# One unread product of the identity ahead of the waits of every piece in a kernel's first edge loop on TensorE

## What is computed

```python
agg = jax.ops.segment_sum(x[src], dst, num_segments=N)
deg = jax.ops.segment_sum(jnp.ones_like(src, dtype=x.dtype), dst, num_segments=N)
mean = agg / jnp.maximum(deg, 1.0)[:, None]
out = mean @ W_l.T + b_l + x @ W_r.T
...
out = jax.nn.relu(out)
```

## Time and profile before

| | |
|---|---|
| time of 3 runs, median (lowest to highest) | 8019.0 us (8017.02 to 8020.97) |
| the profiled execution's own time | 7943.43 us |
| its span | 7941.6 us |
| mean granted TensorE clock over the span | 0.796 |

### The profile page before, as it was taken

One profiled execution on the slowest core, in us unless ns is written; L12 is line 12 of the kernel. 1 busy time (PEld: TensorE's weight loads), 2 busy tenths in 40 slices (PEclk: granted clock), 3 DMA queues, 4 the chain that ended last, 5 costly groups with the idle time before them and its releaser, 6 DMA issues.

```text
span 7941.6 us, 116432 instructions
## 1 busy us (share of the span) xinstructions
PE 5394.5 (68%) x23625; PEld 3970.9 (50%) x23625; DVE 5453.7 (69%) x13210; ACT 2600.2 (33%) x9112; POOL 3724.1 (47%) x3988
## 2 busy tenths in 40 slices
PE   6265666625777776946655555899577777777798
PEld 4143333323444443425555555787455555555687
DVE  8776667776666765546666666764688778778666
ACT  1022222212332231314444444211445554555211
POOL 0266666626666663645555555000444444444211
PEclk8566666766877877967777877999788888888899
DMA  3132333223333432443333333354455555555311
GB/s 109 51 89 82 91 88 89 82 82 109 107 108 112 117 110 83 137 124 111 110 111 107 109 109 110 124 163 132 120 139 140 138 139 138 140 141 139 88 43 38
DMA packets 448815, 865.10 MB, mean 109 GB/s; under 512 B 78232, under 2 KB 284168, under 8 KB 447626
## 3 DMA queue, kind: packets, MB, share of 16 engines
q0 software_dynamic: 194048, 574.45, 26.3%
q1 hardware_dynamic: 237674, 251.25, 10.2%
q10 hardware_dynamic: 16416, 31.99, 1.2%
HBM read 718.55 MB, written 298.46 MB: 128 GB/s over the span
## 4 chain that ended last, share of the span: by engine, by line
PE 30%; DVE 22%; issue 14%; another core or an unknown queue 6%; POOL 3%; SPq 3%; DMA 2%; DVEq 2%; ACT 2%; ACTq 1%; POOLq 0%
PE ps L839 6%; PE ps L1553 4%; PE ps L1818 3%; DVE big L1488 3%; PE ps L1781 3%; SPq L1411 2%; PE ps L2007 2%; PE ps L2024 2%; PE ps L1503 2%; DVE big L1911 2%; DVE big L1927 2%; DVE big L1936 1%; DVE big L786 1%; PE ps L1201 1%
## 5 line engine op out<-in xcount | busy, mean ns | idle before, releaser
L839 PE MATMUL ps<-ring 128*128 x3528 | 1479.7, 545 | 962.0 <-DVE ohb L776 410.9
L839 PEld LDWEIGHTS ps<-ring 128*128 128x128 f32 x3528 | 724.6, 251 | 1457.0 <-issue 1419.8
L1503 PE MATMUL ps<-big,ring 128*128 128x128 f32 x4928 | 875.6, 346 | 599.5 <-DVE big L1478 405.8
L746 POOL DMA_INDIRECT ring<-xl_d,idx x832 | 847.6, 1019 | 715.4 <-DVEq L641 316.0
L813 ACT CAST ring<-ohb 128x128 f32<-128x128 bf16 x1764 | 524.3, 298 | 2003.3 <-DVE ohb L776 1192.7
L1439 POOL DMA_INDIRECT big<-x_d,idx x832 | 793.9, 954 | 747.9 <-ACT ring L1464 506.4
L1503 PEld LDWEIGHTS ps<-big,ring 128*128 128x128 f32 x4928 | 802.5, 250 | 672.5 <-DVE big L1478 455.7
L1689 POOL DMA_INDIRECT ring<-kv_d,gidx x754 | 712.8, 945 | 814.0 <-issue 746.9
L746 POOL DMA_INDIRECT ring<-x_d,idx x832 | 827.7, 995 | 438.2 <-issue 232.7
L776 DVE TENSOR_SCALAR ohb<-iotab,keyf,nbase 128x128 bf16<-128x128 bf16 x1764 | 571.0, 324 | 462.6 <-remote 161.4
L786 DVE TENSOR_TENSOR big<-big,ps 128x257 f32 (+1 forms) x1764 | 754.1, 428 | 170.1 <-issue 108.1
(11 more groups left out here) (413 smaller groups left out, 9283.0 us busy)
## 6 DMA issues: line engine op xcount, KB each, us to landing
bas_d<-big SPq DMA_DIRECT2D x1232, 128.0 KB
att_d<-wreg SPq DMA_DIRECT2D x464, 132.0 KB
big<-bas_d SPq DMA_DIRECT2D x49, 1024.0 KB, 5.6
x_d<-ring SPq DMA_DIRECT2D x147, 128.0 KB, 1.7
gh_d<-aside ACTq DMA_DIRECT2D x49, 384.0 KB
ring<-xl_d,idx POOLq DMA_INDIRECT x832
ring<-x_d,idx POOLq DMA_INDIRECT x832
big<-x_d,idx POOLq DMA_INDIRECT x832
```

The lines of the kernel that those rows point to most:

```text
L746: nc.gpsimd.indirect_dma_start(out=rows[:, j, :], out_offset=None, in_=table, in_offset=bass.IndirectOffsetOnAxis(ap=idx_of(c), axis=0)).t ...
L839: T.matmul(ps[k][:, 0:D], ohf[:, k, :], rows[:, slot, :].rearrange("p a d -> p (a d)"), start=True, stop=True)
L1503: last = nc.tensor.matmul(ps[j % 8][:, 0:FW].rearrange("p (n h b) -> p n h b", n=NB, h=H)[:, :, h, :], xs[:, j, h * P:(h + 1) * P], wts[:, ...
```

## The change

In the first edge loop (`layer` is 0) TensorE makes one product of the identity with itself, 128 x 128 in f32, into bank `ps[7]`, ahead of the waits of each piece. Nothing reads it, and it increments no semaphore. The second edge loop keeps `gates_pe` in that place.

```diff
@@ -830,6 +830,8 @@
                     of[:min(GRP, NQ - q)] = load_group(mybir.EngineType.PE, chunk_i, q, min(GRP, NQ - q), NCK - 1)
                 if layer:
                     gates_pe(pe, q)
+                else:
+                    T.matmul(ps[7][:, 0:P], ident[:, :], ident[:, :], start=True, stop=True)
                 pe.wait_ge(e["oh"], layer * NQ + q + 1)
                 pe.wait_ge(e["arrived"], of[a] + layer * NCK + 1)
                 if past(q, G1):
```

## The result

| | before | after |
|---|---|---|
| median of 8 runs (lowest to highest) | 8023.41 us (8017.02 to 8027.39) | 8043.49 us (8036.59 to 8049.11) |
| the profiled execution's own time | 7943.43 us | 8043.77 us |
| its span | 7941.6 us | 8041.9 us |
| its mean granted clock | 0.796 | 0.810 |

The ratio of the medians is 1.0025, with a 95% interval from 1.0014 to 1.0036: the change costs 20 us, between 11 and 29. The direction and the range were right; the 67 us forecast were more than three times too much. One of the 17 runs of the kernel before in the third batch (8053 us at a mean clock of 0.544) is left out of its ratios as a slow run.

The account below looks back on a forecast made before the run. The prediction held no engine full: TensorE set about a quarter of the first edge loop's time, VectorE and late releases the rest. +94 - 27 = +67 us on 8019 gave 8086, stated as 8085 us, range 7955 to 8230.

Parts of the forecast that it names:

- the clock (0.81 for 0.79): First edge loop: mean granted TensorE clock would rise from 0.69 to 0.79, as in the second edge loop.
- the 1764 records: First edge loop: the 882 added products would show as 1764 matmul records in the changed profile.
- their place in the pauses: First edge loop: products of 263 pieces would fall into TensorE's idle time, 1.8 us on average; few waited for.
- the distances back to back: First edge loop: pieces without a pause would be 0.82 us apart at the upper clock, 1.56 at the lower.
- VectorE's waits put down to the count product: First edge loop: VectorE's waits for L841 would grow from 87 us; the prediction is wrong if they don't.
- mostly at the upper clock: First edge loop: the prediction is wrong if pieces after a pause run mostly at the upper clock; it took 58%.
- TensorE holds 24% of the chain: First edge loop: TensorE's 123 us of a 514 us stretch of the wait chain; gave the +94 us term.
- The 31%: First edge loop: growth of TensorE's cost of a piece back to back, from 0.86 to 1.13 us.
- The 302 us: First edge loop: TensorE's time that paces it, 0.24 x 1257 us, on which 31% would be paid.
- the products of 619 pieces: First edge loop: 619 of 882 pieces start right behind the piece before, so their added product is paid.
- The second term: First edge loop: 263 pieces after a pause fall from 1.01 to 0.91 us by the better clock, -27 us.
- The rule weighed in the prediction: First edge loop: keeping TensorE busy holds the clock up; as the faster rival, -60 us, 7960 us, chance 0.30.

Follow-up runs that it names:

- the third batch: On a quicker chip: unchanged kernel 6891.90 us; against it, the change 0.9994, and an f32 identity product with one column instead of 128 1.0338.

## Why the size was wrong

Right were the clock (0.81 for 0.79), the 1764 records, their place in the pauses (no engine waits for them), the distances back to back to within 7% (0.77 and 1.49 for 0.82 and 1.56), and that the traces show nothing that changes behind the loop. VectorE's waits put down to the count product went from 67 us (53.9 + 13.5) to 93 (90.8 + 1.8), but against the trace that the prediction had, with 87, they hardly grew. Of the pieces that start after a pause, 119 of 196 (61%) start at the upper clock, 114 of 280 before; the prediction had reckoned with 58%, so its sign of being wrong, "mostly at the upper clock", tells nothing either way.

**The step that failed** is "TensorE holds 24% of the chain: 0.24 x 1257 = 302 us of the loop. 31% of that is +94 us". Both of its factors were too large.

*The 31%.* With the measured distances and clock a piece costs 0.62 x 0.77 + 0.38 x 1.49 = 1.04 us against 0.86, 21%, and the same step gives +64. But the clock's share of the time isn't its share of the pieces. From one count product to the next, where TensorE has no idle time between them, it takes 0.869 us at the mean in the kernel before (592 times) and 0.954 in the changed one (681 times), of which 80% are at the upper level and not 62%. That is 10%, and the same step gives **+30 us**. The shown rows agree: TensorE is busy for 800.75 / 882 = 0.91 us a piece before and 905.32 / 882 = 1.03 after, 13% more, the added product included in every piece. Two thirds of the +94 were lost here.

*The 302 us.* The same step for every kernel, once with the measured distances weighted by the loop's clock and once with the measured mean of the pieces back to back, against what was measured on chips of the first kind:

| product ahead of a piece | upper, lower, weighted (us) | by the step | mean in the trace (us) | by the step | measured |
|---|---|---|---|---|---|
| bf16, 1 column | 0.57, 1.09, 0.88 | +8 | 0.87 | -1 | -1 |
| bf16, 512 columns | 0.67, 1.31, 0.93 | +23 | 0.86 | -5 | +9 |
| f32, 128 columns (the change) | 0.77, 1.49, 1.04 | +64 | 0.95 | +30 | +20 |
| bf16, 512 columns, twice | 0.89, 1.73, 1.11 | +87 | 1.01 | +48 | +20 |
| f32, 128 columns, twice | 0.99, 1.92, 1.19 | +117 | 1.12 | +86 | +37 |
| f32, 1 column | -, 1.49, 1.49 | +221 | 1.49 | +217 | +50 |

Where the step by the mean in the trace gives more than the noise, it gives one and a half times to four times what was measured, so no one share of the loop stands for TensorE. What was wrong with the 24% is seen in VectorE's stops: the chain of waits goes from such a stop to the TensorE product that ended last before it was over, while the product waited for had ended 1.8 us or more before, about 7 at the median, in each of 231 stops before and 172 after. VectorE waits for late releases there, not for TensorE's work, and the prediction priced part of them as TensorE's own time. With 301 us of late stops here and 4 on the quicker chip, late releases are also what the 184 us between the two loops come with. By what way the added work still costs 20 us is not shown: VectorE's late stops are 20 us longer in all, but 9 us longer with one bf16 column, which costs nothing.

I had called the products of 619 pieces paid in full because they start right behind the piece before. TensorE's idle time shrank by 88 us for 105 us of work, so most of them ran into a pause that got shorter.

**The second term**, -27 us for 263 pieces after a pause at a better clock, rested on the same full payment. The product behind the waits loads the same pieces with 80 us and costs 6, so by that measure the 27 were worth 2 us, and by the intervals hardly more than 8. It had the other sign and hid part of the first error.

**The clock.** No run shows that its rise gives anything by itself: 0.74 to 0.98 on the quicker chip is 0.9996, but there the gathers pace the loop, and on the first kind of chip no run changes the clock alone. What the columns change is seen in the one-column run: the same f32 instructions without them leave the clock at 0.50 and cost 50 us for 20, and 233 for none. In bf16 it is the other way: 512 columns cost 9 us and one column nothing. The rule weighed in the prediction (the Trainium skill, "TensorE: Matmul & The Clock Gate", section "Why this matters for your kernels": keep TensorE busy and free of pauses) agrees with the changed kernel's trace in the clock, and not in the time: this loop waits for gathers or for late releases. With the f32 product of one column the trace does not agree even in the clock: TensorE is busy by its records for 1317 of 1328 us, and the clock is 0.50.

**Left open.** Why releases come late on some chips and not on others, with one program: medians of 8023 to 8044 us in three of the measurements, 6892 and 6903 in two. The first loop accounts for 184 us (1271 against 1087, with VectorE equally busy, 874 us) of the 1136 between the spans of two traces (8039.8 and 6903.8), the second for 200 (1280 against 1079). By what way the product costs 20 us, by TensorE's time or by its number of instructions. And why the kernel without the count is slower.

## What to carry to other kernels

An added instruction on an engine with pauses is priced by how much of it the idle time takes up, and not by the engine's share of the chain; a step built on that share gave one and a half to four times too much here. Before an engine's share is taken as its price, look whether the waits put down to it end right behind the very instruction waited for. Weight a clock by pieces, not by time, where pieces are what is priced. Move the same work behind the waits once: if that costs nothing either, its engine isn't waited for. The product that raised the clock at the lowest price was one bf16 instruction of 512 columns (0.13 and 0.24 us), and f32 with one column cost as much as with 128 and left the clock at 0.50; in no run here did a raised clock pay for its product. Where the profiled execution lies 1% off the median, take another before costing anything from its rows.

## What the runs showed of the hardware

An f32 product of the identity with one column costs TensorE as much as one with 128, at the lower clock: 1.49 us from piece to piece with either, 1.06 without. In bf16 one column costs 0.03 us.

The same program takes 14% less on some chips than on others. VectorE, ScalarE and GpSimd are as busy on either to within half a percent (VectorE 5458 and 5441 us of the whole span), and TensorE less by its clock. On the slower chips a release of a TensorE product for which VectorE stops reaches it 6 to 8 us after the product's end at the median (in every kernel but the one with one f32 column, where most come within 1.5 us), at the place shown with five more right behind it; on the quicker ones it comes 0.14 us after the end.
